# Edge feature dots on GpSimd and VectorE, and one more high one-hot on ScalarE, in the first sort of a graph kernel

## What is computed

```python
h = x @ Wn.T + bn
e = edge_attr @ We.T + be                       # [12500, 256]
xj = h[src]
a = leaky_relu(sum((xj + e) * attn, -1), 0.01)
a = softmax of a over the edges of one dst
out = relu(segment_sum(xj * a, dst))            # layer 1
x = layernorm(x + out)
mean = segment_sum(x[dst], src) / max(count, 1) # layer 2: edges the other way round
x = layernorm(x + x @ W1.T + b1 + mean @ W2.T + b2)
```

## Time and profile before

| | |
|---|---|
| median of 3 runs | 1409.51 us (1405.2 to 1410.82) |
| the profiled execution's own time | 1417.53 us |
| its span, first to last instruction | 1415.7 us |
| PE busy | 1199.2 us (85%), 6829 instructions |
| DVE busy | 1014.9 us (72%), 3558 |
| ACT busy | 705.8 us (50%), 1643 |
| POOL busy | 750.6 us (53%), 731 |
| mean granted TensorE clock | 0.924 of full speed |

### The profile page before, as it was taken

How to read it: one execution, slowest core, us unless ns; L and a number is a source line. 1 busy time by engine, 2 the same in 40 slices (tenths; PEclk the granted TensorE clock), 3 DMA queues, 4 the chain that set the end, 5 groups by cost and what they waited for, 6 DMA issues and landing times.

```text
span 1415.7 us, 24884 instructions
## 1 busy us (share of the span) xinstructions
PE 1199.2 (85%) x6829; PEld 1043.3 (74%) x6829; DVE 1014.9 (72%) x3558; ACT 705.8 (50%) x1643; POOL 750.6 (53%) x731
## 2 busy tenths in 40 slices
PE   5988968990099999949999999999988888888884
PEld 5977847880078888838888888888877777777773
DVE  8377897888455555349999999999986656565551
ACT  4655564550034444427777766667763343434332
POOL 1047772767767777744444106656532555556533
PEclk9989999995589999979999999999998888988887
DMA  7779885979436666557777778999962332223211
GB/s 232 256 156 218 198 251 160 280 214 362 148 65 93 101 95 93 71 132 247 244 238 243 250 242 297 311 329 323 326 226 60 90 89 92 86 92 92 90 50 40
DMA packets 118168, 254.24 MB, mean 180 GB/s; under 512 B 23705, under 2 KB 63272, under 8 KB 118084
## 3 DMA queue, kind: packets, MB, share of 16 engines
q1 hardware_dynamic: 75738, 187.26, 41.6%
q0 software_dynamic: 40128, 64.45, 20.1%
q10 hardware_dynamic: 2218, 1.53, 0.3%
HBM read 175.67 MB, written 130.44 MB: 216 GB/s over the span
## 4 chain that ended last, share of the span: by engine, by line
PE 71%; DVE 9%; issue 8%; DMA 5%; ACT 4%; POOL 2%; SPq 1%; ACTq 0%; DVEq 0%; POOLq 0%
PE bank L1378 41%; PE bank L1367 8%; PE bank L1355 5%; PE bank L1427 3%; PE bank L1431 3%; PE bank L1521 3%; PE bank L1277 3%; DVE stats L957 3%; DVE X L784 2%; DMA X<-in_x,idx_src 2%; ACT aggn L631 2%; ACT sel L685 1%; PE bank L1314 1%; DVE xin L784 1%; POOL X L482 1%
## 5 line engine op out<-in xcount | busy, mean ns | idle before, releaser
L1378 PE MATMUL bank<-w1T,xT 128*128 128x256 f32 x1968 | 481.3, 392 | 1.8 <-ACT yout L594 1.8
L1378 PEld LDWEIGHTS bank<-w1T,xT 128*128 128x128 f32 x1968 | 379.1, 197 | 55.9 <-ACT xT L584 2.2
L492 POOL DMA_INDIRECT order_scratch<-pay,rank_i x200 | 195.8, 979 | 218.4 <-DVE xin L784 90.3
L589 ACT ACTIVATE std<-stats,eps_c 128x4 f32<-128x4 f32 x271 | 80.5, 298 | 278.0 <-DVE stats L957 278.0
L584 ACT ACTIVATE xT<-bank 128x512 f32<-128x512 f32 x296 | 176.8, 598 | 82.7 <-PE bank L1367 78.1
L594 ACT ACTIVATE yout<-bank,rstd 128x256 f32<-128x256 f32 x492 | 203.9, 480 | 0.7 <-DVE rstd L1023 0.5
L532 POOL DMA_INDIRECT z_scratch<-xin,idx_out x100 | 156.3, 1563 | 53.9 <-ACT xin L711 30.7
L957 DVE BATCH_NORM_STATS2 stats<-bank 128x6 f32<-128x512 f32 x246 | 167.8, 691 | 10.3 <-PE bank L1378 10.2
L957 DVE BATCH_NORM_STATS2 stats<-xin 128x6 f32<-128x512 f32 x240 | 154.6, 685 | 22.1 <-DMA xin<-z_scratch 22.1
L1378 PE MATMUL bank<-w2T,xT 128*128 128x256 f32 x400 | 126.8, 447 | 50.5 <-issue 49.8
L1355 PE MATMUL bank<-sel,agg 128*128 128x196 f32 x800 | 156.2, 339 | 0.0
(11 more groups left out here) (248 smaller groups left out, 1729.3 us busy)
## 6 DMA issues: line engine op xcount, KB each, us to landing
z_scratch<-in_x SPq DMA_DIRECT2D x125, 400.0 KB
xin<-z_scratch SPq DMA_DIRECT2D x97, 512.0 KB
out_rows<-yout SPq DMA_DIRECT2D x97, 512.0 KB, 3.2
kB<-sorted_scratch SPq DMA_DIRECT2D x50, 256.0 KB, 3.5
yout<-low_digits_scratch SPq DMA_DIRECT2D x50, 128.0 KB, 6.6
yout<-keys_scratch SPq DMA_DIRECT2D x50, 128.0 KB, 5.7
yout<-in_edge_attr SPq DMA_DIRECT2D x12, 512.0 KB, 5.8
order_scratch<-pay,rank_i POOLq DMA_INDIRECT x200
```

The costliest lines, as they stand in the source:

```text
L492: g.indirect_dma_start(out=order_dram[k], out_offset=bass.IndirectOffsetOnAxis(ap=rank_i[k][:, t:t + 1], axis=0), in_=pay[:, t, :], in_off ...
L1378: ins = mm(to, buf[:, jj, c, 0:n], w[:, c, :], start=not bias and i == 0 and c == 0, stop=i == len(terms) - 1 and c == 1)
```

## The change

The dots leave TensorE. `u_b` holds u in every partition: the small product is attn_b times weT and gives 128 columns instead of one. Pool waits for the weights (`s_wcp`) and then, chunk by chunk, multiplies the loaded edge features with u_b in place (14 instructions, `s_eap`). VectorE sums each chunk along the features with one tensor_reduce straight into `pay[:, :, 2]` and gives `s_eau` after each. Sums 0 to 6 stand among the DST one-hots, after groups 12, 14, ... 24 (counted from 0); sums 7 to 13 follow `biases`, where `edge_dots` stood. SyncE loads chunk c when sum c - 4 is done, and starts on the low digits after all 14 sums; Pool's first scatter waits for all 14 too. TensorE's turns and dots and ScalarE's copies are gone. In the DST sort ScalarE makes the last two high one-hots of a group instead of the last one (`BY_ACT`), VectorE two instead of three; the SRC sort stays as it was.

```diff
+X_AXIS = mybir.AxisListType.X
+BY_ACT = (2, 1)
...
+    NCH = NEC + FT + 1 - NEC * EC
...
-        u_c = sb("u_c", [P, 1])
+        u_b = sb("u_b", [P, DE])
...
+        def chunk_tile(c):
+            return c * EC if c < NEC else NEC * EC + c - NEC
+
+        def chunk_rows(c):
+            t = chunk_tile(c)
+            return edge_rows[c % 4][0:P if t < FT else LT, 0:EC if c < NEC else 1, :]
...
+        def hots_before(k, q):
+            return BY_ACT[k] * q + (BY_ACT[DST] * Q if k == SRC else 0)
...
-            for c in range(4, NEC + FT + 1 - NEC * EC):
-                sp.wait_ge(s_eaT, 2 * (c - 3))
+            for c in range(4, NCH):
+                sp.wait_ge(s_eau, c - 3)
                 load_edges(c)
                 copy_x(2)
-            sp.wait_ge(s_eaT, Q)
+            sp.wait_ge(s_eau, NCH)
...
-            pool.wait_ge(s_eau, 1)
+            pool.wait_ge(s_wcp, 4)
+            for c in range(NCH):
+                pool.wait_ge(s_ea[c % 4], 16 * (c // 4 + 1))
+                part = chunk_rows(c)
+                n, k = part.shape[0], part.shape[1]
+                g.tensor_tensor(part, part, u_b[0:n, :].unsqueeze(1).to_broadcast([n, k, DE]), ALU.mult).then_inc(s_eap, 1)
+
+            pool.wait_ge(s_eau, NCH)
...
-            a.copy(u_c[:], bank[4][:, 0:1])
+            a.copy(u_b[:], bank[4][:, 0:DE])
...
             def high_onehots(k, q):
-                n = k * Q + q
-                wait(act, s_hotA, n - 3)
-                t = GT * q + GT - 1
...
+                for i in range(BY_ACT[k]):
+                    t = GT * q + GT - BY_ACT[k] + i
+                    n = hots_before(k, q) + i
+                    wait(act, s_hotA, n - 3)
...
                 for q in range(Q):
                     high_onehots(k, q)
-                    if k == DST:
-                        copy_edges(q)
...
-            def edge_dots():
-                then(v.memset(pay[:, FT:T, 2], 0.0))
-                dve.wait_ge(s_ead, Q)
-                v.tensor_copy(pay[:, 0:FT, 2], bank[0][:, 0:FT])
-                v.tensor_copy(pay[0:LT, FT:FT + 1, 2], bank[0][0:LT, FT:FT + 1]).then_inc(s_eau, 1)
+            def edge_dots(c):
+                t = chunk_tile(c)
+                part = chunk_rows(c)
+                n, k = part.shape[0], part.shape[1]
+                if c == NCH - 1:
+                    then(v.memset(pay[:, FT:T, 2], 0.0))
+                dve.wait_ge(s_eap, c + 1)
+                v.tensor_reduce(pay[0:n, t:t + k, 2], part, X_AXIS, ALU.add).then_inc(s_eau, 1)
...
-                    if t % GT < GT - 1:
+                    if t % GT < GT - BY_ACT[k]:
                         ts(onehot_hi[:, t, :], iota16[:, 0:HC], dig_f[k][:, 1, t:t + 1], None, ALU.is_equal)
                     if t % GT == GT - 1:
                         ins.then_inc(s_onehot, 1)
+                        if k == DST and t % (2 * GT) == GT - 1 and t >= 12 * GT:
+                            edge_dots((t - 12 * GT) // (2 * GT))
...
             biases()
-            edge_dots()
+            for c in range((Q - 12 + 1) // 2, NCH):
+                edge_dots(c)
             starts(DST)
...
-                mm(bank[4][:, 0:1], weT[:, b, :], attn_c[:, b:b + 1], start=b == 0, stop=b == 1)
+                mm(bank[4][:, 0:DE], attn_b[:, b, :], weT[:, b, :], start=b == 0, stop=b == 1)
...
                     if t % GT == 0:
-                        if k == DST:
-                            turn_edges(t // GT)
                         pe.wait_ge(s_onehot, k * Q + t // GT + 1)
-                        pe.wait_ge(s_hotA, k * Q + t // GT + 1)
+                        pe.wait_ge(s_hotA, hots_before(k, t // GT + 1))
                     count_tile(hist, t)
-                    if k == DST and t % GT == GT - 1 and t > GT:
-                        dot_edges(t // GT - 1)
-                if k == DST:
-                    dot_edges(Q - 1)
```

More of the change, by code:

```diff
@@ L186, in build @@
         edge_rows = [t[:].rearrange("p j c -> p (j c)").rearrange("p (t d) -> p t d", d=DE) for t in yout]
-        edge_turned = [xT[2 + i][:].rearrange("p a b c -> p (a b c)") for i in range(2)]
         spare16 = aggn[:, 2:4, :].rearrange("p j c -> p (j c)").bitcast(BF16)
@@ L216, in build @@
         s_ea = sems("edge_features_loaded", 4)
-        s_eaT = sem("edge_features_turned")
-        s_eac = sem("edge_features_copied")
-        s_ead = sem("edge_dots_psum")
+        s_eap = sem("edge_products")
         s_eau = sem("edge_dots_ready")
@@ L638, in high_onehots @@
             def high_onehots(k, q):
-                n = k * Q + q
-                wait(act, s_hotA, n - 3)
-                t = GT * q + GT - 1
[L642 to L649, removed]
+                for i in range(BY_ACT[k]):
+                    t = GT * q + GT - BY_ACT[k] + i
+                    n = hots_before(k, q) + i
+                    wait(act, s_hotA, n - 3)
+                    o = gap_hi[n % 4]
+                    made = gap(o, iota16[:, 0:HC], -1.0, dig_f[k][:, 1, t:t + 1])
+                    is_zero(onehot_hi[:, t, :], o, made).then_inc(s_hotA, 1)
             def upper_across(k, q):
@@ L673, in _ @@
                     high_onehots(k, q)
-                    if k == DST:
-                        copy_edges(q)
-                act.wait_ge(s_hotA, (k + 1) * Q)
+                act.wait_ge(s_hotA, hots_before(k, Q))
                 if k == DST:
@@ L1292, in shift_ordered @@
                 mm(o[:, 3 * P:3 * P + T], lastrow[:], keyc[k][:, 0:T], start=True, stop=True).then_inc(s_next, 1)
-            def edge_tiles(g):
-                return range(GT * g, min(GT * g + GT, FT + 1))
-            def edge_rows_of(t):
-                return P if t < FT else LT
-            def turn_edges(g):
-                for t in edge_tiles(g):
-                    c, i = (t // EC, t % EC) if t < NEC * EC else (NEC + t - NEC * EC, 0)
-                    pe.wait_ge(s_ea[c % 4], 16 * (c // 4 + 1))
-                    n, j = edge_rows_of(t), t % GT
-                    if j == 0:
-                        wait(pe, s_eac, g - 1)
-                    ins = tr(bank[3 + g % 2][:, j * P:j * P + n], edge_rows[c % 4][0:n, i, :], ident[0:n, 0:n])
-                ins.then_inc(s_eaT, 1)
-            def dot_edges(g):
-                pe.wait_ge(s_eac, g + 1)
-                for t in edge_tiles(g):
-                    n, j = edge_rows_of(t), t % GT
-                    ins = mm(bank[0][0:n, t:t + 1], edge_turned[g % 2][:, j * P:j * P + n], u_c[:], start=True, stop=True)
-                ins.then_inc(s_ead, 1)
             def sort(k, after):
```

## The result

| | before | after |
|---|---|---|
| median | 1409.47 us beside it | 1425.4 us of 4 (1415.8 to 1432.69) |
| ratio | | 1.0098 [1.0059, 1.0137] |
| a second set, of 12 | 1413.27 us beside it | 1423.37 us, ratio 1.0092 [1.0059, 1.0125] |
| the profiled execution | 1417.53 us, span 1415.7 | 1415.8 us, span 1414.0 |

The change makes the kernel slower by 0.9 to 1.0%, 13 to 14 us by the ratio. The prediction had said 1420 us, within 1403 to 1433. Medians are over all executions, also the few far above the rest (before: two of 23 near 1453 us), which the ratios set aside. One thing must be held apart from the start: the profiled execution of after is 1.7 us *shorter* than that of before. So the stages are read each by itself.

The account below looks back on a forecast made before the run. TensorE bounds the DST stretch until the scans at 70.4 us; afterwards Pool's products holding VectorE's one-hots and late sums put scans at 80, plus 0.3: +10 us on 1409.5, so 1420 us, range 1403 to 1433.

Parts of the forecast that it names:

- TensorE leaves the path: DST stretch: without turns and dots, 1.30 of 1.98 us a group goes, leaving TensorE under 17 us.
- ScalarE's one-hots: DST histogram: 50 one-hots of 0.84 us, 42.0 us, end at 62.6 us; histogram done about 64 us, against 70.4.
- The price of a product: Pool, DST stretch: 2.0 us per 1024-element product, no less than 1 and no more than 3.9.
- Exclusion: DST one-hots: each 2.0 us Pool product stops VectorE's one-hots throughout; eight products add 16 us, one-hots end at 64.3 us.
- The biases: VectorE, after sum 6: weights and biases take 3.8 us, from 65.5 to 69.3 us.
- The tail: After the biases: sum 7 at 70.5, chunk 11 loaded 75.8, multiplied 77.8, summed 79.0, small chunks done at 80 us.
- The shift of the end: From scans to kernel end: the scans' shift is carried through whole, with 0.3 us for the low-digit load, +10 us.
- the last rival: DST look-ups: a later wait for a low-digit load absorbs the shift, time within 5 us of before; chance 0.03.
- No exclusion: DST stretch: products run beside one-hots, scans start at 64 to 65 us, -5 to -6, 1404 us; chance 0.20.
- brief holds: DST one-hots: products hold them for a quarter of the 16 us, scans near 68 to 70, 1408 us; chance 0.15.
- a product of 3.9 us: Pool: product twice as long as forecast, one-hots lose 31 us and loads wait, +30, 1440 us; chance 0.12.
- the first rival: DST stretch: Pool's products do not hold one-hots, scans start at 64 to 65 us, 1404 us; chance 0.20.

Follow-up runs that it names:

- the products cut down: The changed kernel with each Pool product covering one of 128 features, waits, sums and loads kept: 1399.07 us, ratio 0.9904.
- the second one-hot above: The changed kernel with BY_ACT = (1, 1), so ScalarE makes one of four DST high one-hots and VectorE 175: one execution, 1434.83 us.

## Why the prediction was right, point by point

**TensorE leaves the path**: right, by the chain above. With the products cut down the scans start 7.2 us sooner than before, so no other wait stood right behind TensorE's (within 7 us).

**ScalarE's one-hots**, 50 x 0.84, over at 62.6: line L653 of after starts its last at 62.5 us and ends at 63.0.

```profile
L653 ACT ACTIVATE X<-aggn,ones x50: 457/458/459, 21.4 to 62.5; 128x196 bf16<-128x196 bf16 x50
```

**The sums**: 1.2 us forecast, 1.20 measured, beside products too.

**The price of a product**: 2.0 us, from eight affine_selects of 128 elements. It is 2.34 to 2.38, once 2.51.

```profile
L510 POOL TENSOR_TENSOR yout<-yout,u_b x14: 449/2351/2511, 21.1 to 82.9; 128x1024 f32<-128x1024 f32 x12, 128x128 f32<-128x128 f32 x1, 84x128 f32<-84x128 f32 x1
```

The forecast was 15% short. A one-tile product takes 0.45 us where a select of the same size was started every 0.24, so a second input seems to cost nearly as much again on a short instruction (no run has the same operation with one input); that the select's fixed part was counted eight times made up for most of it, as hoped, and the upper bound of 3.9 us was far off. In a sentence apart: the estimate of 2.25 us worked out from the Trainium skill (GPSIMD Engine Reference, elementwise cycle accounting) was the nearer of the two, 4% below the row.

**Exclusion**: the step that decided, and the one with least behind it (one cast at L791). It holds in every run that could have spoken against it: a one-hot beside a Pool instruction lasts as long as that one, whether 0.45, 1.0 or 2.35 us, reading or not; one gets through beside each product or piece, two beside each memset. The Trainium skill's rule (SBUF — State Buffer, who interferes with whom) is borne out by these rows, for tensor_reduce as well, which kept 1.20 us. The short hold beside the affine_selects fits it, with a Pool instruction that is itself short. The count was off both ways: nine products start before the last one-hot, not eight, since sums free buffers early enough for chunk 8; and three of them (44.00, 54.55, 59.60) begin under a sum, while one one-hot passes beside each. 17.1 us were lost against 16 forecast, and one-hots ended at 64.1 against 64.3, with errors that cancel (nine times 2.35 would be 21.2, less what the sums covered and the one-hots that passed).

**The biases** are the step that failed, though the time came out within the range: 3.8 us forecast, 7.4 measured (65.18 to 72.6). I had let the exclusion hold for one-hots and forgotten it for what comes behind them: the addition to w1T took 2.10 instead of 0.49 us beside the product at 64.58, and a scalar_tensor_tensor of three partitions 2.84 instead of 0.74 beside that at 69.36. In the second profiled execution of the changed kernel they took 7.8 us, with other instructions held (a tensor_tensor of three partitions 2.42 us, a cast 2.45). A rule about two engines has to be applied to every instruction that the two share the time with.

**The tail**: sum 7 was to end at 70.5 and ended at 73.8; the load behind it took 4.3 us, one less than assumed. For the small chunks I gave 1 us; they took 2, because SyncE issued each load only behind two copies of x, so that the very last one went out at 77.35, 1.3 us after the sum that freed its buffer. Scans at 83.7 instead of 80.

**The shift of the end**: +10 forecast, with every later us kept. The true path is +13.3 at the scans, of which 3 us are absorbed by the low-digit load and the gathers (the last rival in small, which had a chance of 0.03 as the whole story), +10.1 at the 400th BATCH_NORM_STATS2. There the forecast agrees to a us, and this is luck: one error of +3.7, for the biases and the tail, and one of -3.5, for what was not carried. The step "the shift of the scans is the shift of the end" does not hold in general, by the pairs given with the second one-hot above. The kernel then came out 10 to 16 us longer by the medians and 13 to 14 by the ratios. The 3 to 4 us over the forecast's 10 are less than executions of one kernel differ by (12 of the changed kernel lie between 1415.3 and 1434.01 us), and the clock in the last stage is one cause of this that the traces show.

**Slips in the prediction's sums.** A product of 2.6 us, taken tenfold, gives +16 and not +18, so the forecast's own range should have ended at 1426. The low-digit load's 5.0 against 4.8 us are 0.2 us, not 0.3 (0.3 was measured). The earlier trace rows shows 25 scatters, not 27. Nothing hangs on these.

**The rivals.** No exclusion, brief holds and a product of 3.9 us are refuted by the rows above. The scans of the kernel with the product cut down, at 63.2 us, are near the 64 to 65 that the first rival would have given; its time, 1399 us, is 5 us under that rival's 1404.

## What to carry to other kernels

Before work is moved to an idle GpSimd, list what VectorE runs at that time. Here a product on GpSimd cost VectorE nearly its own length beside one-hots, casts and two-input operations (2.14 us of 2.35); a memset cost it 0.7 of 1.0 us beside one-hots, and nothing beside a two-input operation; beside tensor_reduce, or while VectorE waits, neither costs anything. An element-wise product of 1024 fp32 took 1.25 us on VectorE and took 2.14 from it on GpSimd, so the busy engine was the cheaper place; where the work must go to GpSimd, put it behind the last one-hot. And move only as much as brings the engines level: a third of the dots moved gained 0.4% (on either engine), all of them, with products on GpSimd beside the one-hots, lost 1%.

## What the runs showed of the hardware that was not expected

- A GpSimd memset that reads nothing excludes VectorE's one-hots as a product does (0.98 to 1.14 us for each of two one-hots beside a memset of 1.0 us), but not a scalar_tensor_tensor with two inputs in SBUF: 0.74 us beside a memset, 2.84 beside a product.
- The turns go by instruction and not by time or size: a 3-partition cast takes 2.46 us beside a 128-partition product instead of 0.41, and between two products or pieces that stand back to back one one-hot gets through. Pool waits too: a product that begins under a scalar_tensor_tensor takes 2.88 us instead of 2.36.
- TensorE's granted clock can stay at half for 58 us in a stretch where, in another execution of the same kernel, it was 18.5 of 20 us busy at full clock. With the same program one of six executions took 1416 us, one 1432 and four 1442 to 1446.
- In the last stage the clock is at half for about a quarter of the time (0.85 in the mean), but in the two profiled executions of the changed kernel this stopped before the end, and 12 us were gained. Whether that follows from the change or from chance stays open: the other experiments' profiled executions show 0.85 in their last 116 us (one 0.87), among them one that ends 17 us later and one that ends 24 us later, and the changed kernel's timed executions spread over 19 us.
